# A segment scan in software-pipelined steps: the memory update one step sooner, the q feature before its rotation, other orders on ScalarE and GpSimd

## The reference

```python
def step(carry, inp):
    mem, z = carry
    q_s, k_s, v_s, qn_s, kn_s = inp          # q_s, k_s rotated; qn_s, kn_s not
    sdpa = softmax(mask(q_s @ k_s.T * SCALE)) @ v_s
    sq, sk = elu(qn_s) + 1, elu(kn_s) + 1
    mem_out = (sq @ mem) / (sq @ z + 1e-06)
    out = beta * mem_out + (1 - beta) * sdpa
    prev_v = (sk @ mem) / (sk @ z)
    mem = mem + sk.T @ (v_s - prev_v)
    z = z + sk.sum()
```

## Time and profile before

| | |
|---|---|
| median of 3 runs | 3200.29 us (3196.45 to 3203.32) |
| the profiled execution, own time | 3204.32 us |
| its span | 3202.6 us |
| the scan's steps | from 1787 us to the end |
| busy in the span | PE 2712.7, DVE 2519.8, ACT 1863.9, POOL 1743.2 us |

### The profile page before, as it was taken

One profiled execution on the slowest core, in us unless ns is written; L12 is line 12 of the kernel. 1 busy time (PEld: TensorE's weight loads), 2 busy tenths in 40 slices (PEclk: granted clock), 3 DMA queues, 4 the chain that ended last, 5 costly groups with the idle time before them and its releaser, 6 DMA issues. The chain is left out here.

```text
span 3202.6 us, 129385 instructions
## 1 busy us (share of the span) xinstructions
PE 2712.7 (85%) x53553; PEld 1539.1 (48%) x53553; DVE 2519.8 (79%) x7597; ACT 1863.9 (58%) x3797; POOL 1743.2 (54%) x1984
## 2 busy tenths in 40 slices
PE   5775999999999999976241599999999989999998
PEld 2332333333333333355131366666666666666665
DVE  3556888888888888856734588888888888888886
ACT  4565688888888888842000355455555545555553
POOL 4664122222222222232045588888888888888885
PEclk9877799999999999997565799999999999999999
DMA  3557434333343333257013000000000000000000
GB/s 108 200 180 243 97 92 95 99 90 87 91 101 95 92 92 93 67 161 228 3 36 90 12 5 11 11 11 11 11 11 11 11 11 11 11 5 11 11 8 10
DMA packets 179264, 209.94 MB, mean 66 GB/s; under 512 B 28593, under 2 KB 140145, under 8 KB 178417
## 3 DMA queue, kind: packets, MB, share of 16 engines
q1 hardware_dynamic: 176112, 200.25, 22.7%
q0 software_dynamic: 2560, 1.35, 0.4%
HBM read 125.10 MB, written 75.63 MB: 63 GB/s over the span
## 5 line engine op out<-in xcount | busy, mean ns | idle before, releaser
L792 ACT ACTIVATE at_pA<-at_ps 128x512 f32<-128x512 f32 x1024 | 563.0, 605 | 45.3 <-DVE at_ps L845 44.0
L845 DVE TENSOR_TENSOR at_ps<-at_ps,w_ratio 128x128 f32<-128x128 f32 (+3 forms) x1024 | 470.9, 494 | 129.3 <-PE at_ps L689 128.7
L664 POOL TENSOR_SCALAR_AFFINE_SELECT at_pB<-at_pB 128x128 f32<-128x128 f32 x256 | 74.8, 292 | 752.5 <-ACT at_pB L798 752.5
L854 DVE CUSTOM_DVE_ANT_0 at_junk<-at_ps,w_cmask 128x512 f32<-128x512 f32 (+3 forms) x1024 | 459.5, 486 | 2.5 <-PE at_ps L695 0.8
L798 ACT ACTIVATE at_pB<-at_ps 128x512 f32<-128x512 f32 (+1 forms) x768 | 376.6, 530 | 113.5 <-PE at_ps L702 110.2
L689 PE MATMUL at_ps<-at_aq,at_ak 72*128 72x512 bf16 x1024 | 338.2, 392 | 39.7 <-DMA at_ak<-parts_scratch 35.1
L1943 POOL TENSOR_TENSOR sc_rb<-sc_rb,v_sin 128x512 f32<-128x512 f32 x256 | 326.1, 1274 | 37.8 <-DVE sc_ra L2183 36.2
L689 PEld LDWEIGHTS at_ps<-at_aq,at_ak 72*128 72x128 bf16 x1024 | 101.1, 99 | 401.9 <-DVE at_mx L854 111.0
L1979 PE MATMUL sc_ps<-sc_xT,v_wqkv 128*128 128x512 f32 x512 | 286.4, 641 | 2.7 <-PEq L56 1.4
L722 PE MATMUL at_ps<-at_pA,at_v 128*32 128x512 f32 x2048 | 277.2, 613 | 0.0
L1938 POOL TENSOR_TENSOR sc_sk<-sc_ee,sc_relu 128x512 f32<-128x512 f32 x128 | 166.6, 1302 | 187.4 <-ACT sc_ee L2133 187.4
(11 more groups left out here) (316 smaller groups left out, 6076.2 us busy)
## 6 DMA issues: line engine op xcount, KB each, us to landing
parts_scratch<-fr_parts SPq DMA_DIRECT2D x64, 384.0 KB, 4.1
at_bq<-parts_scratch SPq DMA_DIRECT2D x192, 96.0 KB
at_bk<-parts_scratch SPq DMA_DIRECT2D x192, 96.0 KB
at_aq<-parts_scratch SPq DMA_DIRECT2D x192, 96.0 KB
at_ak<-parts_scratch SPq DMA_DIRECT2D x192, 96.0 KB
v_scratch<-fr_v SPq DMA_DIRECT2D x32, 352.0 KB, 4.3
at_v<-v_scratch SPq DMA_DIRECT2D x32, 352.0 KB, 3.5
parts_scratch<-fr_parts SPq DMA_DIRECT2D x32, 256.0 KB, 3.9
```

The source lines that it names most:

```text
L792: act.activation(pA[:, n % A_RING, j * S:(j + 1) * S], src, ACT.Exp).then_inc(exped, 1)
L845: dve.tensor_tensor(src[:, 0:wide], src[:, 0:wide], W["ratio"][:, S - wide:S], ALU.mult).then_inc(tilted, 1)
L854: ins = dve.tensor_tensor_reduce(junk[:, P * j * (j + 1) // 2:P * (j + 1) * (j + 2) // 2], src[:, col:col + wide], W["cmask"][:, S - wide: ...
```

## The change

Four orders are changed; no operation is added, dropped or given another shape.

1. The memory update (PE L2003, DVE L2199) of a piece is made at step p+3, not p+4, at the same place in the step. PE's waits are adapted: the update now waits for `skc` of its own piece, and waits for `mu` count one piece more.
2. DVE makes the q feature (`sigma_q`) ahead of the q rotation (`rope`). The q bank is then free when the rotation has been read (`rp`), not when the feature has been (`sgq`).
3. ACT copies v before `skN`, makes `features` of k before the scores' exponential, and copies `oT` before `yT`.
4. POOL subtracts the recalled v at the end of its step, not between the k feature and the k rotation.

```diff
@@ POOL
                         if s < PT:
                             sigma_k(s)
-                        p = s - 2
-                        if inside(p):
-                            new = uu[:, p % PAIRS, :, :, 0:DH]
-                            wait(pool, "kd", p + 1)
-                            wait(pool, "pvd", p + 1)
-                            pool.tensor_tensor(new, new, t1[...], ALU.subtract).then_inc(G["ud"], 1)
                         if s < PT:
                             rotate(2 * s + 1)
...
                             pool.tensor_tensor(o, o, t2[...], ALU.add).then_inc(G["od"], 1)
+                        p = s - 2
+                        if inside(p):
+                            new = uu[:, p % PAIRS, :, :, 0:DH]
+                            wait(pool, "kd", p + 1)
+                            wait(pool, "pvd", p + 1)
+                            pool.tensor_tensor(new, new, t1[...], ALU.subtract).then_inc(G["ud"], 1)
@@ PE
                             wait(pe, "pt", p + 1)
+                            wait(pe, "v_c", p + 1)
                             local(p)
...
-                            wait(pe, "mu", 2 * min(s - 5, PT - 1) + 1)
+                            wait(pe, "mu", 2 * min(s - 4, PT - 1) + 1)
                             wait(pe, "sgk", p + 1)
                             recall(p, 1, "kr_s")
...
-                            wait(pe, "mu", 2 * min(s - 5, PT - 1) + 2)
+                            wait(pe, "mu", 2 * min(s - 3, PT))
                             wait(pe, "add_d", 2 * p + 2)
                             score(p)
...
-                        p = s - 4
+                        p = s - 3
                         if inside(p):
                             wait(pe, "qd", min(s - 1, PT))
                             wait(pe, "sx", min(s, PT))
-                            wait(pe, "mu", 2 * p)
                             wait(pe, "ud", p + 1)
+                            wait(pe, "skc", p + 1)
                             update(p)
@@ ACT
                             features(2 * s)
+                        if s < PT:
+                            act.copy(uu[...], ps[:, bank_of("v", s), :]).then_inc(G["v_c"], 1)
                         p = s - 1
                         if inside(p):
                             act.copy(skN[...], ps[:, 6, :]).then_inc(G["skc"], 1)
                         if s < PT:
-                            act.copy(uu[...], ps[:, bank_of("v", s), :]).then_inc(G["v_c"], 1)
+                            features(2 * s + 1)
                         p = s - 1
                         if inside(p):
                             act.activation(ss[:, p % 2], ss[:, p % 2], ACT.Exp).then_inc(G["se"], 1)
-                        if s < PT:
-                            features(2 * s + 1)
@@ DVE
                         if s < PT:
+                            sigma_q(s)
+                        if s < PT:
                             rope(2 * s)
-                        if s < PT:
-                            sigma_q(s)
...
-                        p = s - 4
+                        p = s - 3
                         if inside(p):
                             update(p, 0)
```

More of the change, by code:

```diff
@@ L2058, in _ @@
                             wait(pe, "otc", min(s - 3, PT))
+                            if s >= PT:
+                                wait(pe, "skc", min(s - 1, PT))
+                                wait(pe, "old", min(s - 2, PT))
                             wait(pe, "pt", p + 1)
+                            wait(pe, "v_c", p + 1)
                             local(p)
@@ L2064, in _ @@
                         if inside(p):
-                            wait(pe, "mu", 2 * min(s - 5, PT - 1) + 1)
+                            wait(pe, "mu", 2 * min(s - 4, PT - 1) + 1)
+                            if s >= PT:
+                                wait(pe, "qd", min(s - 2, PT))
+                                wait(pe, "kd", min(s - 2, PT))
                             wait(pe, "sgk", p + 1)
@@ L2070, in _ @@
                             wait(pe, "old", min(s - 1, PT))
+                            if s >= PT:
+                                wait(pe, "otc", min(s - 3, PT))
+                                wait(pe, "skc", min(s - 1, PT))
                             wait(pe, "sgk", p + 1)
@@ L2074, in _ @@
                         if inside(p):
-                            wait(pe, "mu", 2 * min(s - 5, PT - 1) + 2)
+                            wait(pe, "mu", 2 * min(s - 3, PT))
+                            if s >= PT:
+                                wait(pe, "sx", min(s - 1, PT))
                             wait(pe, "add_d", 2 * p + 2)
@@ L2137, in _ @@
                             features(2 * s)
+                        if s < PT:
+                            wait(act, "vp", s + 1)
+                            wait(act, "up", s - PAIRS + 1)
+                            act.copy(uu[:, s % PAIRS, :, :, 0:DH], ps[:, bank_of("v", s), :].rearrange("p (g h d) -> p g h d", h=2, d=DH)).then_inc(G["v_c"], 1)
                         p = s - 1
@@ L2143, in _ @@
                         if s < PT:
-                            wait(act, "vp", s + 1)
-                            wait(act, "up", s - PAIRS + 1)
-                            act.copy(uu[:, s % PAIRS, :, :, 0:DH], ps[:, bank_of("v", s), :].rearrange("p (g h d) -> p g h d", h=2, d=DH)).then_inc(G["v_c"], 1)
+                            features(2 * s + 1)
                         p = s - 1
@@ L2150, in _ @@
                             act.activation(ss[:, p % 2], ss[:, p % 2], ACT.Exp).then_inc(G["se"], 1)
-                        if s < PT:
-                            features(2 * s + 1)
+                        p = s - 3
+                        if inside(p):
+                            wait(act, "ott", p + 1)
+                            wait(act, "oproj", p - 1)
+                            act.copy(oT[:, p % 2], ps[:, 6, :]).then_inc(G["otc"], 1)
                         p = s - 4
@@ L2157, in _ @@
                             act.copy(yT[:], ps[:, 7, :]).then_inc(G["yt_c"], 1)
-                        p = s - 3
-                        if inside(p):
-                            wait(act, "ott", p + 1)
-                            wait(act, "oproj", p - 1)
-                            act.copy(oT[:, p % 2], ps[:, 6, :]).then_inc(G["otc"], 1)
+                        for j in at_step(s, 5):
+                            take_x(act, bank_of("x", j), j, j)
+                        for j in at_step(s, 6):
+                            take_xq(act, bank_of("xq", j), j, j)
                         for j in at_step(s, 3):
```

19 lines of the change are left out of this document (10 added, 9 removed).

## The result

The changed kernel takes 3218.74 us (median of 5 runs, 3216.73 to 3224.31) against 3200.29 us (5 runs, 3196.45 to 3203.32). The ratio is 1.0059, with a 95% interval of 1.0045 to 1.0074: slower by 0.6%, some 19 us. The profiled execution has a span of 3217.0 us.

What follows compares the result with a forecast made beforehand. The prediction took PE's own work as the bound, and DVE in rounding steps; -1.2 - 2 + 16 + 3 = +16 us on the median gave 3216 us, range 3196 to 3235.

Steps and rivals of the forecast that it cites:

- What bounds the kernel: In the scan, PE's own work is a step's floor; in rounding steps DVE is the bound and PE waits for it.
- The collisions, +16 us: In rounding steps, DVE's rounding and POOL operations exclude each other, delaying the update: +16 us, bounded by half and 26.
- The lower bound: Half of the +16 us in rounding steps, if "issue" time PE would have had anyway falls into the wait.
- The clock, +3 us: After longer PE waits in rounding steps, two more falls to the lower clock: +3 us, between 0 and 12.
- The tail, -1.2 us: At the scan's end one update falls out of the last step but one, so PE transposes `yT` sooner: -1.2 us.
- POOL's order, -2 us: The k rotation comes one operation sooner, so PE's scores get inputs sooner: -2 us, bounds 0 and -21.
- the rival "faster": Scores wait for POOL's k rotation, hidden in PE's "issue" time at L2024; some 3185 to 3190 us, chance 0.15.
- q feature before the rotation, "outside the rounding steps 0": POOL's q rotation starts one DVE operation later; outside rounding steps the scores' cover of 0.6 us makes it cost 0.
- ACT's order: The k features no longer wait for the scores' exponential, which comes later but still before DVE needs it: 0.
- the cover of 0.8 us: Time claimed between the scores' later exponential on ACT and DVE's transposition of its result: 0.8 us.
- a bound of 5 us: ACT's later `yT` copy delays the normalization and the q feature's exponential: at most 5 us, taken as 0.
- The signs: Trace signs: longer L1572 and L1575, PE's wait before L2003 over 30 us; against: L1575 at 691 ns, DVE waiting for ACT.

Runs made afterwards that it cites:

- e5: The kernel before without the four rounding operations in the scan (ScalarE writes the scaled input itself): ratio 0.9934, -21 us.
- e4: The kernel before with only POOL's new order and the update one step sooner: ratio 1.0018, +6 us.
- e10: The kernel before with DVE's new order in all steps but the 15 rounding steps: ratio 0.9999, 0 us.
- e9: The kernel before with DVE's new order in the 15 rounding steps only: ratio 1.0044, +14 us.
- e1: The kernel before with only DVE's new order, q feature ahead of q rotation, in all steps: ratio 1.0062, +20 us.
- e2: The kernel before with only ACT's new order, without the swap of `oT` and `yT`: ratio 1.0004, +1 us.
- e6: The changed kernel without the four rounding operations in the scan: ratio 0.9935 to the kernel before, -21 us.
- e3: The kernel before with DVE's and ACT's new orders, POOL and the update as before: ratio 1.0086, +28 us.
- e8: The changed kernel with the rounding spread over three steps: ratio 0.9966 to the kernel before, median 3188.0 us.

## Why the prediction was right, and where its terms were off

The prediction was 3216 us, the measured median 3218.7. The mechanism is the one described. Point by point:

- **What bounds the kernel.** PE was the bound, and DVE in the rounding steps. e5 removes the rounding and wins 21 us. In the trace of the kernel before PE waited 19.3 us on it in all 15 steps, and lost 3.4 us of clock behind these waits.
- **The collisions, +16 us.** In the timelines of both kernels PE waited ahead of the update of the rounding steps 19.3 us before and 32.7 after (start of L2003 behind the start of the head transposition L2036, less the usual 0.53, 15 steps): +13.4. DVE's rounding grew by as much, 13.9. The sum is near, the distribution was not: I had eleven steps at +1.2 to +1.7 and four at 0 to +0.3, and step by step the differences run from -0.9 to +2.4 us. The lower bound, "issue" time that absorbs half, did not come true.
- **The clock, +3 us.** This term was three times too small. From the start of the update to the start of the v projection behind it PE takes 3.32 us in a rounding step at full clock. Over the 15 steps the excess was 3.4 us before and 12.4 after: +9.0. Two falls more were forecast, for 3 us; five more came, and two of the seven lasted longer than the others. The mechanism is right, and the size is inside the bounds of 0 and 12.
- **The tail, -1.2 us.** Rows of the last steps, to be read against the earlier trace rows:

```profile
3211.37 0.59 ACT L2181 COPY sc_yT<-sc_ps 128x512 f32<-128x512 f32 x1 [1.58 <-PE sc_ps L2043]
...
3212.10 0.63 PE L2048 MATMUL sc_ps<-v_ident,sc_yT 128*128 128x128 f32 x4 [0.77 <-ACT sc_yT L2181]
3212.76 0.69 DVE L2282 TENSOR_TENSOR sc_y<-sc_y,sc_ps 128x512 f32<-128x512 f32 x1 [1.15 <-PE sc_ps L2048]
```

  From `yT` to the last addition 1.39 us pass, and 2.67 did: -1.28. That term is right.
- **POOL's order, -2 us.** This step failed. Together with the update it costs +6 us (e4), since I let POOL's step end where it had ended ("the last of the seven ends near 14.2 to 14.6") and did not see that the subtraction had been filling a wait: with it moved, POOL idles ahead of the k rotation and is 0.4 us late for the next q rotation. PE's idle time at the scores, from which I took a gain, fell from 21.3 to 19.2 us. In the six traces with POOL's new order it is 17.9 to 20.3 us, in the eight with the old one 19.7 to 24.1, so the 2 us may be real. They are small beside what the order costs in the rounding, and far from what the rival "faster" needed.
- **q feature before the rotation, "outside the rounding steps 0".** Right, by e10. Inside them it costs, alone, 14 us by e9 and 20 by e1, intervals that overlap.
- **ACT's order.** Alone 0, by e2; the cover of 0.8 us held. The q feature now waits 6.8 us for ACT, which costs nothing (e6); that the late `yT` is behind it was not tested. It is 5.9 us in e3 and 0 in e2, so it takes DVE's order as well. I had given it a bound of 5 us and taken 0.
- **The signs.** Most came true: L1572's median went from 796 to 1299 ns, PE's wait to over 30 us and into all 15 steps, POOL's wait for the k feature from 176.5 to 101.9 us, and DVE's transposition doesn't wait for ACT. Two that were to show the forecast wrong came too. L1575's median stayed at 692 ns, where over 1.2 us was forecast: in four steps L1574 took the collision in its place, and the median of one operation doesn't show what the group lost. And a wait for ACT appeared on DVE, ahead of the q feature; the sign didn't tell a wait that holds PE up from one that doesn't.
- **The sum.** The parts that the traces show, +13.4, +9.0 and -1.3, make 21.1 of the 22.5 us by which the scans of the two profiled executions differ; the medians differ by 18.5. Against them stood +16, +3, -1.2 and -2. That the forecast came within 3 us of the median is in part luck: the collisions came out 2.6 us smaller and the clock 6 us larger than their terms. The terms were worked out on the whole change. The single edits don't add up: +20, +1 and +6 make 27, and the whole is +19; e3 and e4 would make 34. What POOL's order and the update give back when DVE's order is there was not tested alone; in the traces the rounding takes 62.5 us in e3 and 56.7 in the change, which is 6 of the 9 us between them.

The Trainium skill's rule (SBUF — State Buffer, Who interferes with whom), by which L1574 too excludes a GpSimd operation, was not borne out or refuted before. The trace now agrees in that: L1574 takes 1.65 us where L1938 stood ahead of it. In the other direction, which the prediction had asked about, L1574 holds GpSimd too. In the step at 2543 us of the changed kernel:

```profile
2544.83 0.69 DVE L1574 TENSOR_TENSOR sc_tq<-sc_tq,sc_mq 128x512 f32<-128x512 f32 x1
2545.06 1.58 POOL L1938 TENSOR_TENSOR sc_sk<-sc_ee,sc_relu 128x512 f32<-128x512 f32 x1 [1.01 <-ACT sc_ee L2152]
```

L1938 ends at 2546.64. Less its usual 1.27 us that gives a true start at 2545.37, 0.54 us after the start of L1574, and not only at its end, 0.69 us after; by the earlier trace rows it is the same behind L1575.

## What to carry to other kernels

Where an engine's order is changed in a loop, look for the iterations in which that engine has extra work; an order that is free in 113 steps of 128 cost 14 us through the other 15 (e9). Two engines that exclude each other turn a shift of a few tenths of a microsecond into a wait of a whole operation, and one collision makes the next likely, so read the minimum, median and maximum of one shape before an edit moves anything next to it. To judge the edit, take the time of the whole group: here the median of its last operation did not move while the group lost 13.9 us. And count a wait of PE with the slower clock behind it, which added 9.0 us to 13.4 here. The remedy is not the order that happens to miss: spread the extra work over iterations with idle time, and collisions, though no shorter, cost little.

## What the runs showed of the hardware

All of this is for 128x512 operations between SBUF tiles. A VectorE operation that met a running GpSimd operation ended 0.29 us (L1572, L1573) or 0.55 us (L1574, L1575) after it. Where the GpSimd operation L1938 came second, behind L1574 or L1575, it ended 1.81 us after that operation's start, that is 0.54 us and its own usual 1.27, though it is recorded as started sooner. L1573, in both kernels 0.43 us in every rounding step, was held when its turn came with a GpSimd operation under way: 1.38 us once in e10, and 1.11 us on average in e8. And TensorE's clock fell in seven rounding steps of the changed kernel, with waits of 2.1 to 3.2 us, and not in three others with waits of 2.2 to 2.8 us; why is open.
